# Routed experts computed only for the tokens that chose them, by rows scattered to 128-row tiles in DRAM

## What is computed

```python
shared = silu_and_mul(x @ shared_gate_up_w.T) @ shared_down_w.T      # 704 hidden features
shared = shared * sigmoid(x @ sgate_w.T)
routing_weights = softmax(x @ gate_w.T)                              # 16 experts
topk_w, topk_ids = top_k(routing_weights, 4)
for e in range(16):                                                  # 176 hidden features each
    coef = sum(where(topk_ids == e, topk_w, 0))                      # one number per token
    acc += (silu_and_mul(x @ w13[e].T) @ w2[e].T) * coef
out = shared + acc
```

## Time and profile before

| | us |
|---|---|
| median of three runs | 1421.27 |
| the profiled execution | 1423.36 |
| its span, first to last instruction | 1421.6 |
| PE, DVE, ACT, POOL busy | 1346.2, 869.1, 870.9, 824.7 |

### The profile page before, as it was taken

One profiled execution on the slowest core, in us unless ns is written; L12 is line 12 of the kernel. 1 busy time (PEld: TensorE's weight loads), 2 busy tenths in 40 slices (PEclk: granted clock), 3 DMA queues, 4 the chain that ended last, 5 costly groups with the idle time before them and its releaser, 6 DMA issues. The chain is left out here.

```text
span 1421.6 us, 24665 instructions
## 1 busy us (share of the span) xinstructions
PE 1346.2 (95%) x8500; PEld 1204.4 (85%) x8500; DVE 869.1 (61%) x1795; ACT 870.9 (61%) x1764; POOL 824.7 (58%) x710
## 2 busy tenths in 40 slices
PE   5899999999889999998999999999999969999998
PEld 4688888888778888886899999999999957888887
DVE  5777777777755333346777777777777754343334
ACT  4677777777634333334877777777777744333332
POOL 4156667665525555554577766777667534555554
PEclk9999999999989999999999999999999989999999
DMA  2233324232201111121212211222112011111111
GB/s 97 66 75 78 90 70 92 61 86 61 59 23 45 45 44 55 44 78 38 59 60 80 65 53 54 58 79 61 58 52 58 23 41 34 45 44 44 51 48 41
DMA packets 48635, 82.34 MB, mean 58 GB/s; under 512 B 4288, under 2 KB 29888, under 8 KB 48448
## 3 DMA queue, kind: packets, MB, share of 16 engines
q1 hardware_dynamic: 48576, 81.57, 20.2%
HBM read 80.25 MB, written 1.31 MB: 57 GB/s over the span
## 5 line engine op out<-in xcount | busy, mean ns | idle before, releaser
L1111 DVE TENSOR_TENSOR f_h<-f_sc,ps 128x512 f32<-128x512 f32 x112 | 76.3, 682 | 183.5 <-POOL f_sc L1043 183.5
L353 POOL TENSOR_TENSOR ms_a<-m_a,ms_a 128x384 fp32r<-128x384 f32 x128 | 129.9, 1014 | 100.2 <-ACT ms_a L349 100.0
L223 PE MATMUL ps<-xn_hi,fgu_hi 128*128 128x512 f32 x448 | 178.1, 398 | 4.8 <-DVE f_h L1111 4.7
L224 PE MATMUL ps<-xn_lo,fgu_hi 128*128 128x512 f32 x448 | 176.9, 395 | 0.0
L225 PE MATMUL ps<-xn_hi,fgu_lo 128*128 128x512 f32 x448 | 176.8, 395 | 0.0
L1113 DVE TENSOR_TENSOR fh_lo<-f_h,fh_hi 128x512 fp32r<-128x512 f32 x112 | 107.3, 958 | 100.8 <-ACT fh_hi L349 100.8
L992 ACT ACTIVATE f_s<-ps 128x512 f32<-128x512 f32 x112 | 66.9, 599 | 165.4 <-PE ps L225 165.3
L1043 POOL TENSOR_TENSOR f_sc<-f_s,coef_r 128x512 f32<-128x512 f32 x88 | 113.6, 1292 | 70.3 <-ACT f_s L992 70.3
L349 ACT CAST fh_hi<-f_h 128x512 fp32r<-128x512 f32 x112 | 69.2, 618 | 125.0 <-DVE f_h L1111 124.8
L223 PE MATMUL ps<-fd_hi,fh_hi 128*128 128x256 f32 x448 | 127.2, 284 | 0.4 <-DVE fh_lo L1113 0.4
L224 PE MATMUL ps<-fd_lo,fh_hi 128*128 128x256 f32 x448 | 126.7, 283 | 0.0
(11 more groups left out here) (260 smaller groups left out, 4696.6 us busy)
## 6 DMA issues: line engine op xcount, KB each, us to landing
fw_raw<-ffn_w SPq DMA_DIRECT2D x56, 384.0 KB, 3.0
rows_a<-a_rows_d SPq DMA_DIRECT2D x64, 256.0 KB, 4.5
wconv_raw<-b_conv SPq DMA_DIRECT2D x16, 513.0 KB, 3.5
aw_raw<-a_heads SPq DMA_DIRECT2D x32, 256.0 KB, 2.7
wvo_raw<-b_vo SPq DMA_DIRECT2D x16, 512.0 KB, 3.3
rows_b<-b_rows_d SPq DMA_DIRECT2D x32, 256.0 KB, 4.7
wqk_raw<-b_qk SPq DMA_DIRECT2D x16, 256.0 KB, 4.7
x<-xT SPq DMA_DIRECT2D x2, 512.0 KB, 5.1
```

The costliest lines, as they stand in the source:

```text
L223: nc.tensor.matmul(o, w[0], v[0], start=first, stop=False, skip_group_check=True)
L224: nc.tensor.matmul(o, w[0], v[1], start=False, stop=False, skip_group_check=True)
L353: return nc.gpsimd.tensor_tensor(dst[1], src, f32(dst[0]), ALU.subtract).then_inc(sem(done_sem), 1)
L1111: nc.vector.tensor_tensor(f_h[:, c], f_sc[:, c], ps[:, 2 + c, :], ALU.mult).then_inc(sem("f_h"), 1)
```

## The change

The 22 routed tiles go away; the 6 shared ones stay, without the multiplication by the gate on POOL (the gate is now a per-token scalar in the add to x). The routed part becomes this, in each FFN:

1. DVE computes for every token and each of its four choices a slot: expert e owns rows 128e to 128e+127 of a DRAM tensor, and what goes beyond 128 tokens goes to further tiles. There are 16 + 31 = 47 tiles, a fixed number; for these inputs 41 of them hold rows.
2. POOL scatters the 1024 normed rows, with token number and 16 probabilities (276 words), to their slots: 8 blocks x 4 choices = 32 indirect DMAs of 128 rows.
3. When all 32 have landed, SP loads tile after tile (128 rows, eight buffers). Per tile PE turns x (2 transposes), makes gate and up (2 matmuls of 352 columns, plain float32), turns h (2 transposes) and makes the output (2 matmuls of 256 columns, plain float32). For the 31 further tiles PE reads the place of the weights from SBUF into a register. ACT copies x, takes silu and copies y; DVE forms h and copies its transpose.
4. POOL adds each tile's 128 output rows to one of four DRAM sums by an indirect DMA that adds; a sum takes its next tile only when its last one has landed.
5. SP loads the four sums (8 DMAs of 512 KB), DVE adds them to x: 16 adds instead of 4.

All experts' weights (9.7 MB) are loaded to SBUF at the start of each FFN by nine DMAs that ACT issues. The DRAM tiles and sums of both FFNs (22.7 MB) are filled with zeros and dummy numbers by 20 DMAs which SP issues among block A's loads. DVE takes over most low parts of the shared weights from POOL. B's first weights are loaded at routed tile 20. Semaphores are renamed and merged, buffers moved.

```diff
+EXPERTS, TOP_K, E_HIDDEN, S_HIDDEN = 16, 4, 176, 704
+MORE_TILES = 31
+TILES = EXPERTS + MORE_TILES
+XG, YS, CHAINS, W_GROUPS = 8, 4, 4, 4
...
+            for b in range(BLOCKS):
+                for k in range(TOP_K):
+                    nc.gpsimd.indirect_dma_start(slots_d[f], bass.IndirectOffsetOnAxis(ap=slot4_i[:, b, k:k + 1], axis=0),
+                                                 rows[:, b, :], None).then_inc(sem("slots_stored"), 16)
+            for t in range(TILES):
+                pool.wait_ge(sem("e_y"), TILES * f + t + 1)
+                if t >= CHAINS:
+                    added(pool, f, t - CHAINS)
+                nc.gpsimd.indirect_dma_start(sums_d[f][t % CHAINS],
+                                             bass.IndirectOffsetOnAxis(ap=xg[:, t % XG, ROW_ID:ROW_ID + 1].bitcast(U32), axis=0),
+                                             e_y[:, t % YS], None, compute_op=ALU.add).then_inc(sem(f"e_added{t % CHAINS}"), 16)
...
+            for t in range(-1, TILES + 2):
+                if t + 1 < TILES:
+                    e_turn_pe(pe, f, t + 1)
+                if 0 <= t < TILES:
+                    if t >= EXPERTS:
+                        at_w[t % 3] = pe.value_load(w_at_i[0:1, t - EXPERTS:t - EXPERTS + 1], min_val=0,
+                                                    max_val=(EXPERTS - 1) * E_STRIDE)
+                    e_up_pe(pe, f, t, at_w)
+                if 0 <= t - 1 < TILES:
+                    e_turn_h_pe(pe, f, t - 1)
+                if 0 <= t - 2:
+                    e_down_pe(pe, f, t - 2, at_w)
...
+                ins = nc.tensor.matmul(ps[:, 2 + t % 2, 0:2 * E_HIDDEN], e_xT[:, t % 2, k],
+                                       weights_of(w13, t, at_w, k * 2 * E_HIDDEN, 2 * E_HIDDEN),
+                                       start=k == 0, stop=k == KT - 1, skip_group_check=True)
...
+            sp.wait_ge(sem("slots_stored"), 16 * BLOCKS * TOP_K * (f + 1))
+            for t in range(TILES):
+                if t >= XG:
+                    added(sp, f, t - XG)
+                if t >= XG_SEMS:
+                    loaded(sp, f, t - XG_SEMS)
+                sp.dma_start(xg[:, t % XG], slots_d[f][t * P:(t + 1) * P, :]).then_inc(sem(f"xg_loaded{t % XG_SEMS}"), 16)
+                if f == 0 and t == B_EARLY:
+                    b_first_sp(sp)
+            for q in range(CHAINS):
+                added(sp, f, TILES - 1 - q)
+            for c in range(CHUNKS):
+                for q in range(CHAINS):
+                    sp.dma_start(sums[:, q, c * CHUNK_BLOCKS:(c + 1) * CHUNK_BLOCKS],
+                                 sums_d[f][q][c * CHUNK:(c + 1) * CHUNK, :].rearrange("(b p) m -> p b m", p=P)
+                                 ).then_inc(sem(f"sums_loaded{c}"), 16)
...
         def f_last_dve(dve, n, f, c):
-            dve.wait_ge(sem("f_down_done"), f_count(f, "down_done", F_TILES + 1 + c))
-            for b in range(2 * c, 2 * c + 2):
-                nc.vector.tensor_tensor(of_batch_x(b), of_batch_x(b), halves_of(4 + b), ALU.add).then_inc(sem(f"x_updated{n + 1}"), 1)
+            dve.wait_ge(sem(f"sums_loaded{c}"), 16 * CHAINS * (f + 1))
+            for q in range(CHAINS):
+                for b in range(2 * c, 2 * c + 2):
+                    ins = nc.vector.tensor_tensor(of_batch_x(b), of_batch_x(b), sums[:, q, HALF * b:HALF * (b + 1)], ALU.add)
+                    if q == CHAINS - 1:
+                        ins.then_inc(sem(f"x_updated{n + 1}"), 1)
```

More of the change, by code:

```diff
@@ L19 @@
 F32 = mybir.dt.float32
+I32 = mybir.dt.int32
+U32 = mybir.dt.uint32
 FR = mybir.dt.float32r
@@ L872, in build_layer, with routed, gu_split @@
-        F_LATE_D = 1
-        def f_count(f, name, count):
-            return count + f * F_TOTAL[name]
+        HIDDENS = CHUNKS * S_TILES
+        POOL_GU, POOL_D = 3, 2
+        ROUTE = dict(lg=1, shift=2, mask=3, ranks_read=4, slots=5, w_at=6, exp=1, sg=2, lg_T=1, ranks=2)
+        def routed(eng, by, f, what):
+            eng.wait_ge(sem(f"f_route_{by}"), dict(dve=6, act=2, pe=2)[by] * f + ROUTE[what])
+        def gu_split(eng, f, i):
+            if i < POOL_GU:
+                eng.wait_ge(sem("f_gu_split"), POOL_GU * f + i + 1)
+            else:
+                eng.wait_ge(sem("f_gu_split_dve"), (S_TILES - POOL_GU) * f + i - POOL_GU + 1)
@@ L925, in f_pe @@
[L925 to L933 removed]
+            ins.then_inc(sem("f_route_pe"), 1)
+            f_up_pe(pe, f, 1)
+            f_down_pe(pe, f, 0, [0])
@@ new lines, in f_pe @@
+            routed(pe, "dve", f, "mask")
+            chosen = r_gt[:].rearrange("p i e -> p (i e)")
+            nc.tensor.matmul(ps[:, 7, 0:P], tri[:], chosen, start=True, stop=True, skip_group_check=True)
+            nc.tensor.matmul(ps[:, 7, P:2 * P], ones[:], chosen, start=True, stop=True, skip_group_check=True
+                             ).then_inc(sem("f_route_pe"), 1)
+            routed(pe, "dve", f, "lg")
+            routed(pe, "dve", f, "ranks_read")
+            f_down_pe(pe, f, 0, [1])
@@ L934, in f_up_pe @@
+            for i in range(1, S_TILES - 1):
+                f_up_pe(pe, f, i + 1)
+                f_down_pe(pe, f, i)
+            f_down_pe(pe, f, S_TILES - 1)
+            f_experts_pe(pe, f)
+        def f_up_pe(pe, f, i, chunks=range(CHUNKS)):
+            gu_split(pe, f, i)
             for c in chunks:
-                if not (isinstance(i, int) and i == 0):
-                    pe.wait_ge(sem("f_h"), f_count(f, "h", 2 * i + c - 1))
+                if i > 0:
+                    pe.wait_ge(sem("f_h"), HIDDENS * f + 2 * i + c - 1)
@@ new lines, in e_down_pe @@
+        def e_down_pe(pe, f, t, at_w):
+            pe.wait_ge(sem("e_hT"), TILES * f + t + 1)
+            if t >= 2:
+                pe.wait_ge(sem("e_y"), TILES * f + t - 1)
+            for j in range(2):
+                ins = nc.tensor.matmul(ps[:, 6 + t % 2, 0:DM], e_hT[0:HALF_E, t % 2, j],
+                                       weights_of(w2[0:HALF_E], t, at_w, j * DM, DM),
+                                       start=j == 0, stop=j == 1, skip_group_check=True)
+            ins.then_inc(sem("e_down"), 1)
@@ new lines, in e_y_act, with added, f_lgT_act @@
+        def e_y_act(act, f, t):
+            act.wait_ge(sem("e_down"), TILES * f + t + 1)
+            if t >= YS:
+                added(act, f, t - YS)
+            nc.scalar.copy(e_y[:, t % YS], ps[:, 6 + t % 2, 0:DM]).then_inc(sem("e_y"), 1)
+        CHAIN = [len(range(q, TILES, CHAINS)) for q in range(CHAINS)]
+        def added(eng, f, t):
+            eng.wait_ge(sem(f"e_added{t % CHAINS}"), 16 * (CHAIN[t % CHAINS] * f + t // CHAINS + 1))
+        def f_lgT_act(act, f, c):
+            act.wait_ge(sem("f_logits"), CHUNKS * f + c + 1)
+            nc.scalar.copy(lgT[0:LOGITS, cols(c)], ps[0:LOGITS, 4 + c, :]).then_inc(sem("f_lgT"), 1)
@@ L1090, in f_route_dve, with f_choose_dve @@
+        R_WIDE = [P, BLOCKS, EXPERTS]
+        R_FOUR = [P, BLOCKS, TOP_K, EXPERTS]
+        R_TILES = [P, MORE_TILES, EXPERTS]
+        def f_choose_dve(dve, f, step):
+            routed(dve, "act", f, "exp")
             for b in range(BLOCKS):
```

766 lines of the change are left out of this document (467 added, 299 removed).

## The result

The changed kernel takes 1364.32 us (median of four, 1360.7 to 1366.8) against 1421.55 of the kernel before: a ratio of 0.9596, 95% interval 0.9572 to 0.9619, 57 us less. The forecast said faster and put the time at 1395, 26 us less; so the sign and the range hold, and the gain is twice the forecast's.

What follows compares the result with a forecast made beforehand. The prediction took PE to bound the routed part, about 380 of 1421 us. Changes of -13.6 us in the first FFN and -12.5 in the second summed to -26, a median of 1395 us, range 1325 to 1500.

Steps and rivals of the forecast that it cites:

- first tile to first add: Start of the routed tiles in each FFN: a tile's 2.8 us plus 2.5 to drain, 5.3 us.
- until the slots: Router in each FFN, from first logits until DVE knows the slots: 35.7 us, slots at 433 on the trace's clock.
- slots to the first tile: 32 scatters of 1.3 us, landing 3.0, tile load 3.0: first tile at 481 after slots at 433, 48 us.
- last add to the end: FFN end: 18.5 us; second half's adds +4 before the norm in the first FFN, +5.1 in the second.
- The tile's round: Routed tiles: PE sets the round at 2.8 us, near the middle of 1.1 and 4.4; 47 tiles make 131.6 us.
- second reckoning: Routed tile on PE: true FP32 takes four passes, so 4 x 0.56 + 0.52 = 2.8 us.
- The scatters: POOL's 32 indirect DMAs per FFN: 1.3 us each, 41.6 us, all but 11 us hidden by the shared tiles.
- Block A: 20 fill DMAs of 1.1 MB among block A's loads: costed at nothing, 80 us in all if uncovered.
- Adds set the pace: Rival, routed tiles: adding DMAs set the round; gain gone from 3.1 us issue or 12.4 latency; 1461 at 3.5; chance 0.20.
- Low clock: Rival, routed tiles: PE's clock falls, 4.4 to 5.0 us a tile, +150 to +207, near 1580; chance 0.09.
- Cheaper matmuls: Rival, routed tiles: plain float32 matmuls cost less, 2.0 us a tile, -75, 1320 us; chance 0.12.
- Scatters starve beside DVE: Rival, POOL's scatters: 2.5 to 3 us each in place of 1.3, +77 to +109, 1472 to 1504; chance 0.14.

Runs made afterwards that it cites:

- run with one pass: Changed kernel with the four matmuls of a routed tile on float32r operands, one expert's weights converted once for every tile: 1313.1 us.
- the last experiment: Version with two sums and late expert weights, but next block's five early loads issued behind the loads of the first FFN's sums: 1343.46 us, against 1342.6.

## Why the prediction came out as it did

The direction was right, and for its reasons: PE was the bound, 186 us of its work per FFN went, and less than that had to be put in. The sum named the right places in the right order. It was 33 us too high (-26 forecast, -59 measured, of the span). In the order of the seams, measured less forecast, both FFNs together (the rows are rounded and add up to -34):

| term | forecast | measured | difference |
|---|---|---|---|
| rounds, 46 in each | 2.8 | 2.46, without the stall | -31 |
| first tile to first add | 5.3 | 9.0, 9.9 | +8 |
| stall in the first FFN | 0 | 5.4 | +5 |
| until the slots | 35.7 | 32.5, 33.0 | -6 |
| slots to the first tile | 48 | 45.8, 45.4 | -5 |
| last add to the end | 18.5, +4, +5.1 | 17.8, 19.1, +3.6, +3.9 | -2 |
| ahead of the first logits, block B, end | 0 | -3.1 | -3 |

- **The tile's round.** This is the step that failed, and it carries the difference: 2.8 us a tile was forecast, 2.46 measured, 31 us over 92 rounds. The mechanism was right (PE's round, hardly a wait around it, nothing cheaper for tiles without rows, the clock kept up). The size was the middle between bounds of 1.1 and 4.4, because no plain float32 matmul stood in the trace; that it agreed with a second reckoning made it look firmer than it was. What was too dear was the single pass: the forecast scaled the 0.23 us between starts of 512-column float32r matmuls to 0.16 for 352 columns and took 0.12 for 256, and that is what a float32r matmul takes (0.16 in the run with one pass). But a quarter of a plain matmul takes less, 0.149 and 0.108. The four plain matmuls came at 2.05 us, not 2.24, and the four transposes at 0.44, not 0.52; the rest of the 0.34 us is 2.76 rounded up to 2.8, and the last rounds, which are shorter. An error of an eighth in one term, times 92, is more than the whole gain that was forecast.
- That second reckoning was the Trainium skill's four passes of true FP32 (FP8 and Floating Point Precision, "TensorE Precision Notes"). The trace agrees with the rule roughly: a plain matmul takes 3.7 times as long as a float32r one of as many columns (0.595 against 0.16 us for 352; 0.43 against 0.12 for 256 make 3.6). The number of passes itself no row shows.
- **First tile to first add.** The forecast drained its pipe in 2.5 us. The first y passes through three rounds' stages, behind a PE that starts the tiles at a low clock after its wait (granted clock 0.50 from 473 to 476 us): the first four transposes take 1.23 us. In the run with half of the scatters, where PE comes to them without a wait at full clock, they take 0.60, and first tile to first add is 7.1 us in both FFNs. So about 2 to 3 us of the 9.0 and 9.9 go with the wait, and the forecast's 5.3 was too short without it as well.
- **Until the slots.** The nine issues on ACT were costed at 3.9 us; the eight for the experts' weights (the ninth loads the router's constants) take 3.8 in the queue, but only 1.5 lay on the path, as the run with them moved shows. The rest wasn't taken apart.
- **The scatters.** 1.27 to 1.33 us each where 1.3 was forecast, and 8.9 us of them stood out behind the shared tiles where the forecast had 11. Halving them took 23 us off, which shows how much had been hidden.
- **The stall.** The forecast called the early loads of block B "as before: nothing". Before, no tile load ran beside them; now the tile loads come behind them. The collision was to be had from the diff.
- **The end of an FFN.** 18.5 us from the last y to the first half's adds; 17.8 and 19.1 from the last add's issue. The second half's +4 and +5.1 came at +3.6 (9.6 us from the first half's adds to the norm's low part, 6.0 before) and +3.9.
- **Block A.** Nothing forecast, nothing measured in the windows: PE is full there. The first logits come 2.6 us earlier all the same (1.1 to 2.6 in the kernels that keep the fills as they are). PE's busy time is already 1.0 us more in the first 40 us (26.24 for 25.20), before any of the fills; why stays open.
- **A slip beside the sum.** "186 us of saved PE work per FFN, then, buy 186 us of others" can't stand beside a gain of 13 us per FFN: by the forecast's own terms it was some 173 us of others.

**The rivals.** *Adds set the pace*: not so. The latency is 4.5 us where four sums give 10, and the issue 1.86 where its stated point was 3.1; but it stands only 0.63 us under PE's round and is the next bound for any cheaper tile. *Low clock*: the mean granted clock is 0.96 in the tiles. *Cheaper matmuls* at 2.0 us: the truth lay between it and the forecast. *Scatters starve beside DVE*: not seen. DVE is busy 21 of the 43 us beside the scatters, and most keep their distance of 1.27 us; a few take 1.5 to 1.8. The Trainium skill's warning (SBUF — State Buffer, "SBUF: two separate sides") found no case in these rows. DVE's work there is nearly all TENSOR_TENSOR and SCALAR_TENSOR_TENSOR, so what its other operations would do to the scatters is not shown. That a DVE operation can wait beside a POOL pass did show, as in the earlier trace rows: in the last experiment a step of DVE on 4 columns takes 1.14 us, its like right behind it 0.16. POOL's timeline and DVE's:

```profile
614.12 1.26 POOL L1885 TENSOR_TENSOR wsum_raw<-wconv_raw 128x512 f32<-128x512 f32 x1
```

```profile
614.26 1.14 DVE L384 SCALAR_TENSOR_TENSOR ln_t<-ln_t,ln_v 128x4 f32<-128x4 f32 x1
615.43 0.16 DVE L385 SCALAR_TENSOR_TENSOR ln_r<-ln_t,ln_r 128x4 f32<-128x4 f32 x1
```

## What to carry to other kernels

When an unknown price is multiplied by a hundred, no argument elsewhere in the sum matters as much: split it to the smallest unit that the trace does show (one pass of so many columns at full clock), and don't take a middle of far bounds for a value. Count the parallel chains from latency over round, here 4.5 / 2.5, so two: each one too many is paid behind the loop, in loads and adds (here 18 us for two). And ask of every transfer left "as before" what new transfer it now stands ahead of, and of every one that is moved which engine's queue waits for it.

## What the chip showed that was not expected

- A plain float32 matmul of 352 columns takes 0.595 us from start to start and has two records; 256 columns take 0.43.
- An adding indirect DMA of 128 rows of 1 KB holds POOL for 1.86 us when another follows and for 1.0 when a pass follows; a scatter of 128 rows takes 1.27. From issue until the next add to the same memory may go it is 4.5 us.
- A plain float32 matmul costs 3.6 to 3.7 float32r matmuls of as many columns, not 4.
- Filling DRAM beside a full PE was free with the DMA engines 59% busy, and cost 1 us per further fill (20 us for 20) when twice as many ran and they were 77% busy.
